# Attention's end on four heads at once: denominators and contexts in one operation each, head 2's value product in halves, another order on POOL, PE and ACT

## The reference

```
Q = x @ Wq.T + bq;  K = x @ Wk.T + bk;  V = x @ Wv.T + bv
attn = softmax(einsum('bqd,bkd->bqk', Q, K) * scale)
context = einsum('bqk,bkd->bqd', attn, V)
out = context @ Wo.T + bo + x
h = h + layernorm(out) * gamma + beta
x3 = layernorm(h)                      # input of the feed-forward block
```

## Time and profile before

| what | us |
|---|---|
| median of 3 runs | 161.25 |
| the runs | 161.13, 161.25, 162.66 |
| the profiled execution, its own time | 161.99 |
| its span, first to last instruction | 160.2 |

### The profile page before, as it was taken

One profiled execution on the slowest core, in us unless ns is written; L12 is line 12 of the kernel. 1 busy time (PEld: TensorE's weight loads), 2 busy tenths in 40 slices (PEclk: granted clock), 3 DMA queues, 4 the chain that ended last, 5 costly groups with the idle time before them and its releaser, 6 DMA issues.

```text
span 160.2 us, 3076 instructions
## 1 busy us (share of the span) xinstructions
PE 149.4 (93%) x1015; PEld 134.7 (84%) x1015; DVE 129.4 (81%) x347; ACT 78.0 (49%) x195; POOL 87.4 (55%) x78
## 2 busy tenths in 40 slices
PE   7989879999998799999999999999999999999970
PEld 2789669999984658889999987999999999989830
DVE  0087999999999899888977765999999999892491
ACT  2124965201015789952034314677777777841040
POOL 3063899999999874002777720056454455542050
PEclk9999999999999999999999999999999999999995
DMA  5999999984980000000288129999899994001604
GB/s 165 280 401 401 274 204 274 203 90 72 173 147 2 0 0 6 0 0 0 58 286 330 58 66 280 383 397 377 270 352 284 327 309 166 33 33 30 220 0 115
DMA packets 19554, 28.30 MB, mean 177 GB/s; under 512 B 4839, under 2 KB 14194, under 8 KB 19539
## 3 DMA queue, kind: packets, MB, share of 16 engines
q1 hardware_dynamic: 16918, 21.42, 43.0%
q0 software_dynamic: 1696, 5.52, 14.7%
q10 hardware_dynamic: 924, 1.17, 2.6%
HBM read 19.67 MB, written 5.28 MB: 156 GB/s over the span
## 4 chain that ended last, share of the span: by engine, by line
PE 36%; POOL 23%; DVE 18%; DMA 11%; issue 7%; ACT 1%; SPq 0%; DVEq 0%; POOLq 0%
PE psum L754 13%; PE psum L742 12%; POOL xs_rows L497 8%; POOL prod L357 7%; DMA xT_s<-xT 4%; DVE prod L345 4%; PE psum L714 3%; PE psum L533 3%; POOL wu_l L482 2%; DVE psum L1218 2%; POOL wu_l L478 2%; DMA ys_rows<-yb,xid 2%; DMA wring<-ys_rows 2%; DVE stats L1144 2%; PE psum L729 2%
## 5 line engine op out<-in xcount | busy, mean ns | idle before, releaser
L507 POOL DMA_INDIRECT ys_rows<-yb,xid x22 | 21.5, 978 | 26.0 <-ACT yb L1101 26.0
L1091 ACT ACTIVATE wu<-psum,wring 128x128 f32<-128x128 f32 x92 | 26.0, 371 | 9.5 <-PE psum L742 8.3
L1411 DVE SCALAR_TENSOR_TENSOR tb<-psum,wring,wu 128x128 f32<-128x128 f32 x92 | 25.9, 345 | 0.8
L754 PE MATMUL psum<-wring,tb 128*128 128x128 f32 x184 | 24.8, 278 | 0.1
L742 PE MATMUL psum<-xTb,wring 128*128 128x128 f32 x184 | 24.3, 275 | 0.0
L497 POOL DMA_INDIRECT xs_rows<-xT_s,slot x14 | 14.0, 1000 | 17.2 <-DVE slot L1343 13.2
L754 PEld LDWEIGHTS psum<-wring,tb 128*128 128x128 f32 x184 | 22.3, 191 | 0.6 <-DVE tb L1411 0.3
L742 PEld LDWEIGHTS psum<-xTb,wring 128*128 128x128 f32 x184 | 22.4, 192 | 0.5 <-issue 0.5
L625 PE MATMUL psum<-prod,ident_s 128*128 128x196 f32 (+1 forms) x120 | 21.6, 341 | 1.1 <-POOL prod L345 1.1
L625 PEld LDWEIGHTS psum<-prod,ident_s 128*128 128x128 f32 x120 | 21.1, 190 | 1.2 <-issue 1.2
L357 POOL TENSOR_TENSOR prod<-es,vt 128x3136 f32<-128x3136 f32 x3 | 19.4, 6461 | 0.2 <-ACT es L977 0.2
(11 more groups left out here) (182 smaller groups left out, 278.9 us busy)
## 6 DMA issues: line engine op xcount, KB each, us to landing
wring<-wexp SPq DMA_DIRECT2D x23, 514.0 KB, 4.7
wu<-raw POOLq DMA_DIRECT2D x2, 1536.0 KB, 11.6
raw<-wsh SPq DMA_DIRECT2D x2, 768.0 KB, 9.6
xs_rows<-zero_s SPq DMA_DIRECT2D x1, 1472.0 KB, 15.8
ys_rows<-zero_s SPq DMA_DIRECT2D x1, 896.0 KB, 19.1
xT_s<-xT SPq DMA_DIRECT2D x2, 384.0 KB, 6.0
wu<-wsh SPq DMA_DIRECT2D x1, 768.0 KB, 8.4
xb<-xs_rows SPq DMA_DIRECT2D x1, 585.0 KB, 6.4
```

Of the source, the lines that this page charges most:

```text
L507: pool.indirect_dma_start(ys_dram, bass.IndirectOffsetOnAxis(ap=xid[:, j:j + 1], axis=0), yb[:, j % NY, :], None)\
L754: ins = mm(ps[Y_BANK][:, 0:D], tb[:, j % NTT, c, :], wring[:, j % NR, W2 + c * P:W2 + (c + 1) * P], start=(c == 0), stop=(c == HC - 1))
L1091: ins = A(eb[:, j % NEB, c, :], ps[U_BANKS[j % NU]][:, c * P:(c + 1) * P], ACT.Exp, bias=wring[:, j % NR, B1 + c:B1 + c + 1])
L1411: ins = V.scalar_tensor_tensor(tb[:, j % NTT, c, :], ps[U_BANKS[j % NU]][:, c * P:(c + 1) * P], wring[:, j % NR, B1 + c:B1 + c + 1], eb[:, ...
```

## The change

- DVE sums the denominators of heads 0 to 2 in one operation behind head 3's softmax, head 3's alone, and inverts all four at once. The contexts of two heads come out of one operation; for that the four sums lie in the neighbouring PSUM banks 4 to 7.
- POOL makes the value product of head 2 in two halves of 7 rows, and DVE sums it in two halves.
- PE computes the values of the second pair of heads ahead of the scores of head 1; ACT copies them ahead of head 1's exponential.
- ACT copies the second part of the turned contexts ahead of the high part of the middle weights.
- Three memsets move on DVE from the end of attention to behind the statistics of h2's first group.
- On POOL all six `inv_std` stand ahead of the second half of `wu03_l`, and the first of them ahead of the first half; DVE waits for that second half at `form(0)`.

The diff, cut:

```diff
@@ -43,9 +43,10 @@
 POOL_PV = (0, 1, 2)
 E_OUTER = (1, 3)
 S_INNER = (1, 2)
+PV_PARTS = {0: (range(T),), 1: (range(T),), 2: (range(0, T // 2), range(T // 2, T))}
...
 E_BANK = {3: 1}
-O_BANK = (5, 7, 4, 6)
+O_BANK = (4, 5, 6, 7)
...
-        def product_pv(engine, h):
+        def product_pv(engine, h, rows=range(T)):
...
+                n, part = len(rows), slice(rows[0], rows[-1] + 1)
+                e_ap = weight(h)[:, part].rearrange("p r (o s) -> p r o s", o=1).broadcast_to([P, n, DH, T])
...
-                product_pv(pool, hd).then_inc(S(f"pv{hd}"), 1)
+                for part in PV_PARTS[hd]:
+                    product_pv(pool, hd, part).then_inc(S(f"pv{hd}"), 1)
@@ -477,15 +480,13 @@
...
             outer = [t.rearrange("p g n -> p (g n)") for t in (wu03_l[:, 1], raw02[:, 1], wu_h[:, 3])]
+            inv_std(1, 0)
             for k in range(2):
                 part = slice(k * 3 * DHID // 2, (k + 1) * 3 * DHID // 2)
                 pool.tensor_tensor(*(t[:, part] for t in outer), ALU.subtract).then_inc(S("wu_l_pool"), 1)
                 if k == 0:
-                    inv_std(1, 0)
-            for k in (1, 2):
-                inv_std(1, k)
-            for k in range(len(GROUPS)):
-                inv_std(2, k)
+                    for n, j in ((1, 1), (1, 2), (2, 0), (2, 1), (2, 2)):
+                        inv_std(n, j)
             pool.wait_ge(S("wu_h_done"), 3)
             pool.tensor_tensor(wu12_l[:, 0], wu12[:, 0], wu_h[:, 1], ALU.subtract).then_inc(S("wu1_l"), 1)
@@ -635,14 +636,14 @@
...
+            pe.wait_ge(S("k_done"), 2)
+            values(1)
             pe.wait_ge(S("q_done"), 1)
             scores(1)
-            pe.wait_ge(S("k_done"), 2)
-            values(1)
             scores(3)
-            pe.wait_ge(S("v_done"), 2)
+            pe.wait_ge(S("sub_done"), 1)
             contexts(0)
-            pe.wait_ge(S("sub_done"), 2)
+            pe.wait_ge(S("v_done"), 4)
             contexts(3)
@@ -652,7 +653,7 @@
...
-            pe.wait_ge(S("inv_done"), 4)
+            pe.wait_ge(S("inv_done"), 1)
@@ -984,16 +985,15 @@
...
                 A(wu_h[:, m], raw02[:, k], ACT.Copy).then_inc(S("wu_h_done"), 1)
-            exps(1)
             values(1)
-            exps(2)
-            exps(3)
+            for hd in (1, 2, 3):
+                exps(hd)
...
             context_rows(0)
+            context_rows(1)
             act.wait_ge(S("wu_sum"), 32)
             A(wu_h[:, 1], wu12[:, 0], ACT.Copy).then_inc(S("wu_h_done"), 1)
-            context_rows(1)
...
                 act.wait_ge(S("rstd_done"), ln_count(1, k))
...
-            act.wait_ge(S("wu_l_pool"), 3)
+            act.wait_ge(S("wu_l_pool"), 1)
@@ -1192,24 +1192,36 @@
...
-            def denominator(h):
-
-                dve.wait_ge(S("exp_done"), h + 1)
-                link(V.tensor_reduce(sden[:, h, :], weight(h), AX.X, ALU.add))
-                V.reciprocal(sden[:, h, :], sden[:, h, :]).then_inc(S("inv_done"), 1)
-
-            def context(h):
...
-                                ALU.mult).then_inc(S("ctx_done"), 1)
...
-            def sum_inner(h):
-
-                dve.wait_ge(S(f"pv{h}"), 1)
-                V.tensor_reduce(context_sum(h).rearrange("p (r e) -> p r e", e=DH),
...
+            def denominators():
+
+                dve.wait_ge(S("exp_done"), 3)
+                V.tensor_reduce(sden[:, 0:3, :], es[:, 0:3, :].rearrange("p h (r s) -> p h r s", s=T), AX.X, ALU.add)\
+                    .then_inc(S("den_done"), 1)
+
+            def inverses():
+
+                V.tensor_reduce(sden[:, 3, :], weight(3), AX.X, ALU.add).then_inc(S("den_done"), 1)
+                dve.wait_ge(S("den_done"), 2)
+                V.reciprocal(sden[:], sden[:]).then_inc(S("inv_done"), 1)
+
+            def contexts(pair):
+
+                a = 2 * pair
+                for hd in (a, a + 1):
+                    dve.wait_ge(S(f"o_sum{hd}"), len(PV_PARTS[hd]) if hd in S_INNER else 1)
+                dve.wait_ge(S("inv_done"), 1)
+                V.tensor_tensor(ctx_s[:, a * RW:(a + 2) * RW].rearrange("p (h r e) -> p h r e", h=2, e=DH),
+                                psum[:, O_BANK[a]:O_BANK[a] + 2, 0:RW].rearrange("p h (r e) -> p h r e", e=DH),
+                                sden[:, a:a + 2, :].rearrange("p h (r o) -> p h r o", o=1).broadcast_to([P, 2, T, DH]),
+                                ALU.mult).then_inc(S("ctx_done"), 2)
+
+            def sum_inner(h, k=0):
+
+                rows = PV_PARTS[h][k]
+                dve.wait_ge(S(f"pv{h}"), k + 1)
+                part = slice(rows[0], rows[-1] + 1)
+                V.tensor_reduce(context_sum(h).rearrange("p (r e) -> p r e", e=DH)[:, part],
+                                pv[:, h, :].rearrange("p (r e s) -> p r e s", e=DH, s=T)[:, part], AX.X, ALU.add)\
                     .then_inc(S(f"o_sum{h}"), 1)
 
@@ -1229,31 +1241,23 @@
...
             softmax_in(1)
-            denominator(0)
             score_inner(2)
             softmax_in(2)
-            denominator(1)
             dve.wait_ge(S("s_mm3"), 1)
             softmax_in(3)
-            denominator(2)
+            denominators()
             dve.wait_ge(S("v_done"), 4)
             dve.wait_ge(S("exp_done"), 4)
             product_pv(V, 3).then_inc(S("pv3"), 1)
-            denominator(3)
+            inverses()
             sum_inner(1)
-            for hd in (0, 1):
-                dve.wait_ge(S(f"o_sum{hd}"), 1)
-                context(hd)
-            dve.wait_ge(S("sub_done"), 1)
-            sum_inner(2)
-            for hd in (2, 3):
-                dve.wait_ge(S(f"o_sum{hd}"), 1)
-                context(hd)
-            V.memset(rT9[:, 0, 0, :], 0.0).then_inc(S("zeroed"), 1)
-            V.memset(rT9[:, NT + 1, 1, :], 0.0).then_inc(S("zeroed"), 1)
-            V.memset(both[:, NT, :], 0.0).then_inc(S("zeroed"), 1)
-            V.memset(ps[EPS_BANK][:, EPS_COL:EPS_COL + NT], EPS).then_inc(S("zeroed"), 1)
-            dve.wait_ge(S("zeroed"), 4)
+            contexts(0)
+            dve.wait_ge(S("sub_done"), 2)
+            for k in range(2):
+                sum_inner(2, k)
+            contexts(1)
+            V.memset(ps[EPS_BANK][:, EPS_COL:EPS_COL + NT], EPS).then_inc(S("eps_set"), 1)
+            dve.wait_ge(S("eps_set"), 1)
             dve.wait_ge(S("o_mm"), 1)
             ln_stats(1, o_ps, 0)
             scaled_less_mean(0)
@@ -1265,13 +1269,17 @@
...
                 ln_stats(2, h2_ps, k)
+                if k == 0:
+                    V.memset(rT9[:, 0, 0, :], 0.0).then_inc(S("zeroed"), 1)
+                    V.memset(rT9[:, NT + 1, 1, :], 0.0).then_inc(S("zeroed"), 1)
+                    V.memset(both[:, NT, :], 0.0).then_inc(S("zeroed"), 1)
...
             for k in (1, 2):
                 normalise(k)
-            dve.wait_ge(S("wu_l_pool"), 3)
+            dve.wait_ge(S("wu_l_pool"), 1)
@@ -1296,6 +1304,7 @@
 
             dve.wait_ge(S("xp_zero"), 2)
             dve.wait_ge(S("xp_done"), len(LN_GROUPS))
+            dve.wait_ge(S("wu_l_pool"), 3)
             form(0)
             form(1)
             low_part(0)
```

More of the change, by code:

```diff
@@ L345, in product_qk @@
             return engine.tensor_tensor(o_ap, q_ap, k_ap, ALU.mult)
-        def product_pv(engine, h):
+        def product_pv(engine, h, rows=range(T)):
             if h in S_INNER:
-                e_ap = weight(h).rearrange("p r (o s) -> p r o s", o=1).broadcast_to([P, T, DH, T])
-                v_ap = vt[:, h, :].rearrange("p (o e s) -> p o e s", o=1, s=T).broadcast_to([P, T, DH, T])
-                o_ap = pv[:, h, :].rearrange("p (r e s) -> p r e s", e=DH, s=T)
+                n, part = len(rows), slice(rows[0], rows[-1] + 1)
+                e_ap = weight(h)[:, part].rearrange("p r (o s) -> p r o s", o=1).broadcast_to([P, n, DH, T])
+                v_ap = vt[:, h, :].rearrange("p (o e s) -> p o e s", o=1, s=T).broadcast_to([P, n, DH, T])
+                o_ap = pv[:, h, :].rearrange("p (r e s) -> p r e s", e=DH, s=T)[:, part]
             else:
@@ L1193, in softmax_in @@
                                 ALU.subtract).then_inc(S("sub_done"), 1)
-            def denominator(h):
-                dve.wait_ge(S("exp_done"), h + 1)
-                link(V.tensor_reduce(sden[:, h, :], weight(h), AX.X, ALU.add))
-                V.reciprocal(sden[:, h, :], sden[:, h, :]).then_inc(S("inv_done"), 1)
-            def context(h):
-                dve.wait_ge(S("inv_done"), h + 1)
-                V.tensor_tensor(head(ctx_s[:], h), context_sum(h).rearrange("p (r e) -> p r e", e=DH),
-                                sden[:, h, :].rearrange("p (r o) -> p r o", o=1).broadcast_to([P, T, DH]),
-                                ALU.mult).then_inc(S("ctx_done"), 1)
@@ L1208, in sum_inner @@
-            def sum_inner(h):
-                dve.wait_ge(S(f"pv{h}"), 1)
-                V.tensor_reduce(context_sum(h).rearrange("p (r e) -> p r e", e=DH),
```

(5 more changed lines are left out.)

## The result

The changed kernel took 164.3 us in the median (163.69 to 165.07, 4 runs), the kernel before beside it 161.95 (161.13 to 163.1, 4 runs): ratio 1.0175, 95% interval 1.0128 to 1.0222. The forecast was 162.7, in a range of 161.3 to 163.3; the direction and the place were right, the time lies above the range. The profiled execution took 164.07 us, span 162.3. In every ratio of this document, executions more than 1.5% above the fastest of the same kernel are left out on both sides.

What follows compares the result with a forecast made beforehand. Bound by POOL's chain at attention's end with DVE and PE equally late, then DVE's forms. 0.36 us gained up to the last `rstd`, 1.78 lost at `form(0)`: 1.42 on the median 161.25 gives 162.67 us, range 161.3 to 163.3.

Steps and rivals of the forecast that it cites:

- What holds `form(0)`: DVE's first form stands still until POOL's middle split ends at 63.28, then ends at 64.30: 1.42 us later.
- the two engines do not stop each other: Rival at `form(0)`: POOL and DVE run side by side, the 0.36 us gain stays, 160.89 us; chance 0.10.
- work at half pace: Rival at `form(0)`: the form runs at half pace beside POOL, about 0.5 us late, 161.8 us; chance 0.07.
- the third: Rival at attention's end: head 2's sum waits for POOL, so halving its product gains 1.7 us, 160.97 us; chance 0.03.
- my two pieces of evidence: Two trace overlaps with POOL: a DVE operation on 2 numbers taking 1.00 us, and the first form taking 1.29 us.
- Behind `form(0)` nothing absorbs it: From the form through PE's products, expert choice, scatter and experts, everything moves by the same 1.42 us.
- Scores and denominators: Head 3's value product on DVE starts 0.1 us sooner, bounds 0.15 later and 0.3 sooner.
- Inverses and contexts: DVE at attention's end: 56 inverses add about 0.04 us, joint contexts take 0.58 instead of 0.69; first statistics at 48.6.
- The gain up to the last `rstd`, 0.36: DVE begins h2's second statistics sooner, so POOL's last `rstd` ends at 58.08 instead of 58.44; bounds 0.1 and 0.5.
- The range: Whole kernel: 161.3 to 163.3 us, taking in the half pace and leaving out the first and third rival.
- 0.74 off: The profiled execution, 161.99 us, ran 0.74 long against the median 161.25; differences were carried over to the median.
- a rival at 0.02: Wide operations or halves exceed their bounds, or PE's products slow in a longer pause: 162.9 to some 164 us; chance 0.02.

Runs made afterwards that it cites:

- e4: Changed kernel without POOL's split of the middle weights; ACT copies the weights to its place: 161.33 us, ratio 1.0007 to the kernel before.
- e2: Changed kernel with POOL's order of the kernel before, all else as changed: 161.99 us, ratio 1.0032 to the kernel before.
- e3: Kernel before with only POOL's new order and its waits: median 164.97 us of 13 runs, ratio 1.011 from the five shortest.
- e9: e2 with the contexts computed one head at a time: 161.86 us, one run.
- e10: e9 with the denominators and inverses of heads 0 and 1 early, ahead of head 3's softmax: 160.84 us, one run.
- e1: The changed kernel once more, unaltered: 166.05 us in the median of 7 runs, ratio 1.0194 to the kernel before.
- e11: The changed kernel unaltered, on one chip beside e13: 162.91 to 168.42 us, ratio 1.0115 to the kernel before.
- e13: Kernel before, with PE's first expert-body product also waiting for the second half difference's high part: 162.57 to 166.88 us, ratio not given.

## Why the prediction was wrong, point by point

*What holds `form(0)`: right, to some 0.03 us.* The form waited for the running split and ended 1.02 behind it; e4, without the split, sets it free, e2 and e3 show that POOL's order alone decides it. The Trainium skill, SBUF — State Buffer, section "SBUF: two separate sides", has a VectorE operation with two inputs in SBUF and a GpSimd operation that reads SBUF exclude each other: the one that starts first keeps the shared ports for its whole instruction. The trace agrees, with 3.10 us for 1.15 us of work. No semaphore is involved: the form had been issued 2.08 us before the split's end, so what the section on the chip says, that the engines wait for each other through semaphores alone, is too narrow. The rivals in which the two engines do not stop each other, or work at half pace, are out; so is the third, since head 2's sum starts at 44.22 behind the joint contexts and doesn't wait for POOL. One of my two pieces of evidence was not of this kind: the operation on 2 numbers reads one operand in SBUF and not two, and why it stood still is not shown here.

*Behind `form(0)` nothing absorbs it: right.* 1.90 us at the form's end (64.09 - 25.53 against 62.88 - 26.22), 1.89 at the body, and the stretch to the last scatter is as long as before.

*Scores and denominators: right.* The wait for head 3's sum (0.88) and the wide sum (0.76 for 0.75 forecast) are there; head 3's value product starts at 10.44 (35.97 - 25.53) for 10.37 forecast.

*Inverses and contexts: wrong, and the step that failed: the term was mis-sized.* I had 0.5 us gained at the first statistics; 0.11 was lost. The step "adds about 0.04 us" for the inversion of 56 numbers failed first: it took 0.50 us, where 14 numbers take 0.24 in this row of the kernel before:

```profile
35.21 0.24 DVE L1199 RECIPROCAL sden<-sden 128x14 f32<-128x14 f32 x1
```

I had no slope for that operation and took it as nearly all start. The second was the joint context: costed by width alone (0.58; it took 0.62 and 0.63), while it also waits 0.20 us for head 1's sum. e9 and e10 give 0.25 and 0.27 back, together 0.52 of the 0.61 missing; as e10 moves half of the sums of the denominators as well, its 0.27 is not the inversion's alone.

*The gain up to the last `rstd`, 0.36: wrong here, though e3 has it.* The first `rstd` freed on POOL is worth just that alone (31.15). With the joint operations on top the last `rstd` is at 31.60, since the second group then waits 0.47 us for PE: the second half of the attention output, forecast 0.14 sooner, ends 0.48 later (50.97 - 25.53 against 51.18 - 26.22), the same 0.6 us as above. So the shift at the body is 1.89 instead of 1.42.

*The range: wrong at its upper end.* The result, 164.3, lies 1.63 us above 162.67. The profiled execution, at 164.07, is 0.66 above the 163.41 forecast for it: 0.47 is the mis-sized term, the rest start and end of the run. The other 0.97 is how executions lie about their medians. I took 0.74 off since the profiled execution of the kernel before lay that much above a median of three runs; a fourth (163.1) moved that median by 0.70, to 161.95, and the changed kernel's profiled execution lay 0.23 below its median. So the 0.3 us that I allowed for medians to wander was too little.

*The pause of PE: a cost that I left out.* I let it cost its own length; that wide operations cost more than their bounds, or that PE's products slow down in a longer pause, stood under a rival at 0.02. The inversion had no bounds and did cost more, and the products did slow down. In about half of the executions (10 of 19) the pause costs more, 2.40 us by the medians and 4.4 to 4.6 in the profiled ones. In the result itself that had little part: one of four runs (165.07, mean clock 0.977) looks like that kind, and the median of the other three is 164.07, still above the range. With both pauses filled the changed kernel takes 1.0084 and 1.0102 of the kernel before, and the forecast, 162.67 of 161.25, was 1.0088: as a ratio it would have held without the clock, as a time not in this measurement.

## What to carry to other kernels

Moving work out of the way on GpSimd needs a look at what it then meets: here a VectorE operation with two SBUF operands stood still until the running GpSimd operation was done, so long splits belong where VectorE reads at least one operand from PSUM (its value product kept 3.42 us with POOL busy beside it). A price taken from another operation's slope is a guess: look for a row of the same operation at two sizes, or give the term bounds. A joint operation waits for the last of its inputs and delays everything that wanted the first, so its price is the wait as well as the width. And a new pause of TensorE costs more than its length if the clock falls behind it: give it a chance of its own in the range, and fill it if it can't be avoided.

## What the hardware showed that I had not expected

- RECIPROCAL on 128 partitions: 0.24 us for 14 numbers (before), 0.33 for 28 (e10), 0.50 for 56 (changed), so 6.2 ns an element, where a sum reduction costs 1.03.
- The granted clock fell to the 1.2 GHz level behind pauses of PE of 1.42 and 0.31 us (e1, e11), and came back some 10 us later, with PE busy 2.00 of 2.00 in the slices between; behind the same pauses, and one of 1.89 us (e13), it stayed at 1.00 in other executions.
